# One bias operation for both heads, behind the step's last row maximum

## The reference

```
q, k, v = xn @ wq.T + bq, xn @ wk.T + bk, xn @ wv.T + bv     (16 heads of 64)
scores  = q k^T / 8, with -inf above the diagonal
probs   = softmax(scores)            (row maximum, exp, row sum)
attn    = (probs @ v) @ wo.T + bo
```

## Time and profile before

| | |
|---|---|
| median of 3 runs | 2406.46 us (2405.56 to 2408.3) |
| span of the profiled execution | 2400.4 us |
| its own time | not listed apart from the runs; its span is 6.1 us below the median |
| attention pairs | about 80 to 1945 us of the span |
| busy: TensorE | 2271.6 us (95%) |
| busy: VectorE, ScalarE, GpSimd | 1675.7, 1741.4, 1633.9 us (70%, 73%, 68%) |
| mean granted TensorE clock | 0.983 |

### The profile page before, as it was taken

How to read it: one execution, slowest core, us unless ns; L and a number is a source line. 1 busy time by engine, 2 the same in 40 slices (tenths; PEclk the granted TensorE clock), 3 DMA queues, 4 the chain that set the end, 5 groups by cost and what they waited for, 6 DMA issues and landing times. The chain is left out here.

```text
span 2400.4 us, 70752 instructions
## 1 busy us (share of the span) xinstructions
PE 2271.6 (95%) x28666; PEld 1448.5 (60%) x28666; DVE 1675.7 (70%) x4148; ACT 1741.4 (73%) x2380; POOL 1633.9 (68%) x1291
## 2 busy tenths in 40 slices
PE   6999999999999998899999999999999679999996
PEld 4566667575757655557575757575766445455453
DVE  8487777777777766566666666666676846777777
ACT  6577777877777766677777777777787846666665
POOL 3588888888888876678788888888898822222221
PEclk9999999999999999999999999999999889999998
DMA  8699999999999999999999999999999986656662
GB/s 244 124 196 202 194 211 207 196 203 204 209 197 197 208 200 198 198 200 193 174 195 181 189 183 187 185 184 185 182 192 195 232 169 155 165 153 174 149 168 79
DMA packets 1414420, 447.44 MB, mean 186 GB/s; under 512 B 1391664, under 2 KB 1392064, under 8 KB 1414096
## 3 DMA queue, kind: packets, MB, share of 16 engines
q1 hardware_dynamic: 1414096, 442.92, 99.7%
HBM read 67.95 MB, written 41.94 MB: 46 GB/s over the span
## 5 line engine op out<-in xcount | busy, mean ns | idle before, releaser
L1051 POOL TENSOR_TENSOR hl<-probs,hl 128x1024 f16<-128x1024 f32 x544 | 1166.6, 2151 | 350.2 <-ACT hl L903 348.1
L896 ACT ACTIVATE probs<-s_ps,exp_bias 128x1024 f32<-128x1024 f32 (+7 forms) x768 | 633.3, 854 | 316.5 <-DVE exp_bias L730 309.7
L725 DVE TENSOR_REDUCE neg_max<-s_ps 128x1 f32<-128x1024 f32 (+7 forms) x768 | 675.8, 904 | 169.2 <-PE s_ps L526 169.1
L903 ACT ACTIVATE hl<-probs 128x1024 f16<-128x1024 f32 x544 | 575.0, 1057 | 90.2 <-DMA pt<-hl 74.1
L549 PE MATMUL o_ps<-v,pt 128*128 128x65 f16 x4352 | 431.1, 193 | 50.2 <-DMA pt<-hl 43.8
L549 PEld LDWEIGHTS o_ps<-v,pt 128*128 128x128 f16 x4352 | 400.5, 96 | 79.3 <-DMA pt<-hl 36.9
L526 PE MATMUL s_ps<-nat 64*128 64x512 f16 (+3 forms) x3840 | 410.1, 351 | 25.9 <-ACT probs L896 22.4
L550 PE MATMUL o_ps<-v,pt 128*128 128x65 f16 x4352 | 431.4, 194 | 0.0
L551 PE MATMUL o_ps<-v,pt 128*128 128x65 f16 x4352 | 430.2, 192 | 0.0
L550 PEld LDWEIGHTS o_ps<-v,pt 128*128 128x128 f16 x4352 | 399.8, 97 | 19.1
L551 PEld LDWEIGHTS o_ps<-v,pt 128*128 128x128 f16 x4352 | 400.3, 98 | 0.0
(11 more groups left out here) (185 smaller groups left out, 3580.9 us busy)
## 6 DMA issues: line engine op xcount, KB each, us to landing
w_raw<-in_w_pairs SPq DMA_DIRECT2D x48, 576.0 KB, 4.8
o_scratch<-o_hl SPq DMA_DIRECT2D x128, 128.0 KB, 2.6
out<-result SPq DMA_DIRECT2D x31, 512.0 KB, 3.1
x_in<-in_x SPq DMA_DIRECT2D x27, 512.0 KB, 4.9
pt<-hl SPq DMA_TRANSPOSE x544, 5.2
xn_scratch<-xn SPq DMA_DIRECT2D x16, 512.0 KB, 3.8
xn<-in_x SPq DMA_DIRECT2D x11, 512.0 KB, 3.8
x_in_c<-in_x SPq DMA_DIRECT2D x10, 512.0 KB, 3.9
```

The lines of the kernel that those rows point to most:

```text
L725: nc.vector.tensor_reduce(neg_max[:, step.round, acc, h:h + 1], s_ps[(n + h) % S_RING][:, first:end], AX_X, ALU.max, negate=True).then_inc ...
L896: last = nc.scalar.activation(probs_of(n)[:, cols], s_ps[n % S_RING][:, cols], ACT.Exp, bias=exp_bias[:, step.round, acc, h:h + 1], scale= ...
L903: nc.scalar.activation(hl_of(n, 0), probs_of(n), ACT.Copy).then_inc(p_hi_done, 1)
L1051: nc.gpsimd.tensor_tensor(hl_of(n, 1), probs_of(n), hl_of(n, 0), ALU.subtract).then_inc(p_lo_done, 1)
```

## The change

VectorE no longer makes a bias operation for each part of each head right behind that head's maxima. It takes the maxima of both heads first, waits for the last one, and then makes the biases of both heads and all parts of the step in a single operation. bias_done now counts steps and not parts of heads, and the exponentials of both heads wait for the same count.

```diff
@@ row_max
-                    for (t, k0, nb, acc), first, end in places:
-                        found += 1
-                        dve.wait_ge(max_done, found)
-                        nc.vector.tensor_scalar(exp_bias[:, step.round, acc, h:h + 1], neg_max[:, step.round, acc, h:h + 1],
-                                                SOFTMAX_SCALE, LOG_P_SCALE, ALU.mult, ALU.add).then_inc(bias_done, 1)
+                accs = slice(min(part[3] for part in step.parts), max(part[3] for part in step.parts) + 1)
+                dve.wait_ge(max_done, found + 2 * len(step.parts))
+                nc.vector.tensor_scalar(exp_bias[:, step.round, accs, :], neg_max[:, step.round, accs, :], SOFTMAX_SCALE,
+                                        LOG_P_SCALE, ALU.mult, ALU.add).then_inc(bias_done, 1)
@@ row_min
-                dve.wait_ge(bias_done, 2 * parts_before(p, first_step(p, r) + 2))
+                dve.wait_ge(bias_done, NSTEP * p + first_step(p, r) + 2)
@@ exponentials
-                act.wait_ge(bias_done, 2 * parts_before(p, i) + (h + 1) * len(step.parts))
+                act.wait_ge(bias_done, NSTEP * p + i + 1)
```

## The result

The changed kernel takes 2592.86 us (median of 4 runs, 2589.72 to 2594.18) against 2406.01 us before in the same comparison: 1.0777 times the time, 95% interval 1.0763 to 1.079. It is 187 us slower, where 56 had been forecast. The direction was right, the size was not, and the time lies far outside the range of 2440 to 2482.

The account below looks back on a forecast made before the run. TensorE, busy 113.25 of 113.30 us in a regular pair, was taken as the bound. Stalls of 24 (pairs 8-13), 26.5 (0-5), 1.5 (6-7) and 4 us (14-15) sum to 56, added to 2406.46: 2462 us, range 2440 to 2482.

Parts of the forecast that it names:

- the price of the new operation: VectorE's merged bias, 2 or 4 elements wide: taken at 0.15 us each, bounds 0.15 and 0.27, 272 operations.
- The place: Head 0's exponential must wait behind the second head's maxima: 3.9 us a regular pair, 56 us in all.
- lateness: How much later head 0's exponential is ready: 1.14 us in unmasked steps, 1.19 us with two parts.
- room: From head 0's exponential end to the next scores' start, less 0.14 us handover: 0.3 to 0.4 in four steps a pair.
- The waits of the scores: TensorE's scores waiting for exponentials: to grow from 22.4 us to about 75 us, in about 110 waits.
- lateness of 0.9 and 1.3 us: Bounds on head 0's delay: 2.9 and 4.7 us a regular pair, 40 and 72 us for the whole kernel.
- VectorE's saving of 62 us: 272 steps at 0.18 us, 49 us, plus 13 us in 112 two-part steps; all beside TensorE's work.
- The clock falls as well: Rival: granted clock drops to 0.96 in pairs 0 to 13, costing another 65 us, 2527 us; chance 0.05.
- Absorbed more: Rival: only pairs 8 to 13 pay in full and half of 0 to 5, 15 to 40 us; chance 0.10.
- hidden: Rival: every step has enough room for head 0's delay, so the time stays 2406 us; chance 0.03.
- faster: Rival: earlier maxima on VectorE give back TensorE's 22.4 us of waits for exponentials, 2384 us at best; chance 0.04.
- TensorE's waits for transposes: Expected sign in the profile after: these waits fall a little in the last two pairs.

Follow-up runs that it names:

- place alone: Kernel before, with all biases of a step moved behind its last maximum, still 768 one-element operations: 2471.56 us against 2410.24, 1.0258.
- GpSimd shortened: Changed kernel and kernel before, both with GpSimd's low part made for only 32 of 1024 columns: 2458.73 us against 2413.55, one run each.
- width alone: Kernel before, each of the 768 biases at its old position but two elements wide, one an unread filler: 2459.66 us in one run, against 2410.24.

## Why the prediction was wrong

| | regular pair, us | whole, us above its before |
|---|---|---|
| before | 113.3 | 0 |
| place alone | 117.5 | 61 |
| merged, GpSimd shortened in both | 117.3 | 45 |
| width alone, old place | 116.0 | 49 |
| the change | 126.3 | 187 |

**The step that failed** is the price of the new operation: "The new bias operation, 2 or 4 elements wide, I take at the same 0.15 us", with 0.27 as its upper bound. It measured 0.98 us on average and up to 2.09, because it waits for GpSimd, a wait that the prediction doesn't have, in the sum or among the rivals. The rows that I drew on were the one-element bias and the four-wide reduction L739. Neither has the form that the change brings in, a tensor_scalar from SBUF to SBUF with an even number of elements. The trace of before has that form, in groups on which the prediction didn't draw:

```profile
L664 DVE TENSOR_SCALAR x_in<-x_in,moments_a,rstd_a 128x1024 f32<-128x1024 f32 x16 | 22.0, 1373 | 0.0
...
L664 DVE TENSOR_SCALAR nat<-nat,moments_a,rstd_a 128x1024 f32<-128x1024 f32 x4 | 3.2, 806 | 1.0 <-POOL rstd_a L1046 1.0
```

The same line and shape takes 806 ns in the prologue, where GpSimd has little to do, and 1373 ns on average in the pairs, up to 2.62 us. A spread like this within one shape is the sign. The ends show it as well: of the 24 operations on this line 14 take over 0.83 us, and each of these starts under a running GpSimd instruction and ends 546 to 553 ns behind that instruction's end, whatever was left of it. As a bound it would have given 0.15 us plus up to 2.15 us, the length of L1051.

**The place was right.** With lateness 1.14 and 1.19 us and the room at each step the prediction had 3.9 us a pair and 56 us in all: measured in isolation 4.2 and 61 (45 with GpSimd shortened on both sides). Two smaller terms were off. The waits of the scores grow to 97.7 us in 99 with the place alone, where about 75 in 110 had been forecast. And lateness of 0.9 and 1.3 us, put through the prediction's own rooms, gives 2.5 and 4.5 us a pair, not 2.9 and 4.7. VectorE's saving of 62 us did not appear at all in the changed kernel, where it is busy 164 us more. With GpSimd shortened it is 35 us (1620.1 against 1655.2), beside a kernel that is 45 us slower, so it is worth nothing for the time, as argued.

**Why the two parts cost 187 together and not 61 + 49.** The room is used once. With the width alone, head 0 is some 0.7 us late in one-part steps, and most rooms are larger than that. With the place alone it is 1.14 us late, and the rooms of 1.3 us hide that. With both, the wait for GpSimd comes on top of the place. The trace after lets this be worked out step by step. Take the prediction's lateness, add what the step's bias took beyond 0.15 us (0.17 with four elements), subtract the room in the kernel before, and hold the rest against what the next scores waited. Pair 10, in us:

| step | room before | bias after | worked out | waited |
|---|---|---|---|---|
| 1 | 0.33 | 0.45 | 1.14 | 1.09 |
| 6 | 1.33 | 1.21 | 0.87 | 0.79 |
| 7 | 0.94 | 2.09 | 2.14 | 2.06 |
| 10 | 0.33 | 1.38 | 2.07 | 2.03 |
| 12 | 0.42 | 0.30 | 0.90 | 0.86 |
| 15 | 1.43 | 1.62 | 1.18 | 1.10 |
| 16 | 0.42 | 1.53 | 2.13 | 2.08 |

Step 9 has 1.33 us of room too, but its bias took 0.17 us, and nothing waited. Step 13 waited 0.86 us, of which 0.42 is inherited from step 12 as in the prediction; the rest was not worked out. In pair 10 after, the 17 biases take 19.1 us where 17 of 0.15 would take 2.6; the waits of the scores add up to 10.9 us there. The pair is 13.0 us longer: those 10.9, of which 3.9 is what the place alone was forecast to cost, and 2.2 because TensorE is busy 115.43 us for work that took 113.25.

**The rivals.** "The clock falls as well" had 0.05, and part of it came true, behind holes longer than the prediction reckoned with: with the place alone (holes up to 0.87 us) the clock of a regular pair is 1.00, with holes of 2.0 to 2.1 us it is 0.99, and TensorE is busy 2.2 us a pair longer; over the span it is 0.971 against 0.983 in the two profiles (0.974 to 0.980 in the 15 executions of before beside the later runs). "Absorbed more", "hidden" and "faster" all fall. The rule of the Trainium skill (VectorE: DVE Perf Modes, Rules for kernel authors) to minimize the count of chained operations, weighed in the prediction, does not hold for this form: 496 operations fewer, 164 us more busy time on VectorE (1839.5 against 1675.7). TensorE's waits for transposes fell, further than forecast: 8.1 us in 7 waits over the whole span after, 43.8 in 30 before, of which pairs 14 and 15 had 25.9.

**What stays open.** When GpSimd gives the port free where its instructions follow each other closely. Why the width alone meets GpSimd less often in one-part steps (0.85 us for head 0, against 1.11) wasn't separated. A merged bias that takes its maxima from PSUM wasn't measured. Of the 16 us between the 61 and the 45 of the shortened kernels the traces show only where they lie: pairs 8 to 13 cost 25.0 and 23.1 us, nearly the same; pairs 0 to 5 30.4 and 21.1, pairs 6 and 7 2.3 more and 2.0 less, what follows 8.9 and 1.7. The shortened kernels are a single run each.

## What to carry to other kernels

Before merging small operations, look at what form the merged one has, and find a row of exactly that form in the trace, near the engine that will run beside it: here going from one element to two made an instruction of 0.15 us take up to 2.1 us, waiting for GpSimd's work. When many small operations feed another engine, ask for the first consumer's readiness and not for the producer's total. And delays that each fit in the slack can't be added up as free: sum them first, then subtract the room.

## What the runs showed of the hardware

- A VectorE tensor_scalar of two or four elements with input and output in SBUF, and a scalar_tensor_tensor with a second input in SBUF, were held until a GpSimd instruction ended and finished 23 to 32 ns behind it in the changed kernel (15 to 24 with the second input); the wait is booked as VectorE's busy time. One-element instructions were not held, not even inside a running GpSimd instruction (470 such of 768 in the kernel before, 139 to 157 ns).
- With the low part in four instructions and no wait between them, 71 of 232 held biases passed over the end of at least one GpSimd instruction, the longest 4.48 us. With a wait between them 1 of 144 did, and 1 of 227 in the changed kernel.
- Four GpSimd instructions of 256 columns take 4 x 0.68 us where one of 1024 takes 2.15. The kernel before with this change alone took 85 us more in its one run, and nothing more in its regular pairs.
